# Late odd mamba states worked in the PSUM bank of their decays, half by half, on one Trainium2 core

## The reference, cut to what matters

```
x = x + _L1_attn_ref(_layernorm(x), ...)          # this one
def _mamba(x, ...):                               # once forward, once on the reversed sequence
    dA  = exp(dt[..., None] * A)                  # decays, one plane for each of 16 states
    dBx = (dt * xi)[..., None] * Bm[:, :, None, :]
    def step(h, inp):
        a, bx, c = inp
        h = a * h + bx
        return (h, einsum('bds,bs->bd', h, c))
    y = scan(step, 0, ...) + xi * Dp
    y = y * silu(z)
    return einsum('ble,de->bld', y, out_proj)
```

## Time and profile before

| | us |
|---|---|
| median of 3 runs | 2885.27 (2874.43 to 2886.08) |
| span of the profiled execution | 2872.8 |
| PE busy | 2427.9 (85%) |
| DVE busy | 2361.6 (82%) |
| ACT busy | 1705.4 (59%) |
| POOL busy | 1641.3 (57%) |

### The profile page before, as it was taken

How to read it: one execution, slowest core, us unless ns; L and a number is a source line. 1 busy time by engine, 2 the same in 40 slices (tenths; PEclk the granted TensorE clock), 3 DMA queues, 4 the chain that set the end, 5 groups by cost and what they waited for, 6 DMA issues and landing times.

```text
span 2872.8 us, 30435 instructions
## 1 busy us (share of the span) xinstructions
PE 2427.9 (85%) x8581; PEld 887.3 (31%) x8664; DVE 2361.6 (82%) x3470; ACT 1705.4 (59%) x2859; POOL 1641.3 (57%) x1295
## 2 busy tenths in 40 slices
PE   8777767879789897998889887997879898988888
PEld 3232322323322432233222332232322333333222
DVE  2899899888898999999898989989899987255353
ACT  5666546746749484766658485664638372643444
POOL 2787676756737683867747674776838771121201
PEclk9898967989999898999999898998999899999999
DMA  2333331332313241332323232232413331121111
GB/s 95 107 111 104 104 107 60 100 102 86 100 46 118 86 131 36 110 109 88 117 68 108 96 109 63 96 117 82 135 54 123 93 111 34 56 73 62 32 33 38
DMA packets 159384, 251.29 MB, mean 87 GB/s; under 512 B 20088, under 2 KB 58232, under 8 KB 158960
## 3 DMA queue, kind: packets, MB, share of 16 engines
q1 hardware_dynamic: 159216, 249.34, 27.4%
HBM read 231.71 MB, written 16.50 MB: 86 GB/s over the span
## 4 chain that ended last, share of the span: by engine, by line
DVE 28%; PE 25%; issue 16%; ACT 13%; POOL 12%; SPq 2%; DMA 2%; DVEq 0%; POOLq 0%; ACTq 0%; another core or an unknown queue 0%
PE ps L548 25%; DVE nmx L1336 8%; DVE rh L1416 6%; POOL rb L1838 6%; ACT tN L1722 3%; POOL rh L1828 2%; ACT ps L1777 2%; ACT L1463 2%; DMA cr<-shares 2%; SPq L1939 2%; DVE rh L1422 1%; DVE xib L1402 1%; POOL tF L1859 1%; POOL tF L1852 1%; DVE tF L1253 1%
## 5 line engine op out<-in xcount | busy, mean ns | idle before, releaser
L1416 DVE TENSOR_TENSOR_SCAN rh<-ps,rb 128x512 f32<-128x512 f32 x512 | 619.7, 1215 | 91.0 <-ACT ps L1777 82.4
L1336 DVE TENSOR_REDUCE nmx<-ps 128x1 f32<-128x512 f32 (+3 forms) x864 | 530.5, 661 | 55.1 <-PE ps L548 52.6
L1722 ACT ACTIVATE tN<-ps 128x512 f32<-128x512 f32 (+1 forms) x896 | 463.0, 572 | 136.6 <-PE ps L548 119.5
L548 PE MATMUL ps<-tN,strip 128*64 128x512 f32 (+3 forms) x2048 | 469.9, 549 | 2.5 <-DVE hN L1359 1.8
L1838 POOL TENSOR_TENSOR rb<-duf,bs 128x512 f32<-128x512 f32 x256 | 396.6, 1569 | 131.7 <-DVE rh L1416 129.1
L1828 POOL TENSOR_TENSOR rh<-rh,cs 128x512 f32<-128x512 f32 x208 | 315.3, 1519 | 268.7 <-DVE rh L1416 267.1
L1838 POOL TENSOR_TENSOR rb<-dub,bs 128x512 f32<-128x512 f32 x256 | 388.0, 1534 | 63.0 <-DVE rh L1416 43.5
L548 PE MATMUL ps<-hF,W 128*128 128x512 f32 x592 | 341.9, 661 | 57.0 <-DVE tF L1253 29.7
L548 PE MATMUL ps<-Ks,Qs 128*128 128x512 bf16 (+3 forms) x979 | 291.9, 362 | 74.9 <-DVE nmx L1336 66.7
L1852 POOL TENSOR_TENSOR tF<-tF,cr 128x512 f32<-128x512 f32 x128 | 180.8, 1414 | 275.4 <-DVE tF L1257 154.1
L548 PE MATMUL ps<-tF,W 128*128 128x512 f32 x528 | 283.3, 627 | 21.8 <-POOL tF L1859 11.5
(11 more groups left out here) (259 smaller groups left out, 3672.5 us busy)
## 6 DMA issues: line engine op xcount, KB each, us to landing
cr<-shares SPq DMA_DIRECT2D x248, 256.0 KB, 3.3
bs<-rowsf SPq DMA_DIRECT2D x128, 256.0 KB, 3.6
cs<-rowsf SPq DMA_DIRECT2D x128, 256.0 KB, 3.3
bs<-rowsb SPq DMA_DIRECT2D x128, 256.0 KB, 3.6
cs<-rowsb SPq DMA_DIRECT2D x128, 256.0 KB, 3.3
parts<-spl SPq DMA_DIRECT2D x32, 384.0 KB, 2.8
Qs<-parts SPq DMA_DIRECT2D x384, 32.0 KB
Ks<-parts SPq DMA_DIRECT2D x384, 32.0 KB
```

The costliest lines, as they stand in the source:

```text
L548: return eng.matmul(o, l, r, start=start, stop=stop, skip_group_check=skip_group_check)
L1336: red(nmx[:, 4 * qt + 2 * (i // 4) + a, i % 4:i % 4 + k], o[:, 0:k * nk].rearrange("p (k c) -> p k c", k=k), AX.X, ALU.max, negate=True).t ...
L1416: eng.tensor_tensor_scan(rh[n % NH][:, g, :], decays(n, g), rb[n % NBB][:, g, :], 0.0, ALU.mult, ALU.add).then_inc(s_h, 1)
L1722: act(tN[m % NP][:, a, 0:nq], PA[a][:, 0:nq], ACT.Exp).then_inc(s_ex, 1)
```

## The change

Late states are now handled in pairs of an even state n and the odd one behind it, and the other strands do the same work as before.

- The even state is scanned as before into rh, now rh[n // 2 % 3] (`tile_of`), and its product with C is still POOL's, in a strand C of its own, placed by its own letter in the order.
- The odd state is scanned in place: the scan writes PS, over the decays that it reads. Then, in PS and for the same half, DVE multiplies by C (512 columns), adds the even state's rh (join, 512 columns, counted by the new semaphore s_j) and adds the joined half to xi (512 columns). After that comes the next half.
- ACT's exponential into PS waits, behind an odd half, for this last add and no longer for the scan (`bank_free`).
- rh of a pair is free after the join; the waits of the DMAs and of the block's end follow the new counts.
- l1's product is written to the PSUM tile A instead of y, and the add to X reads it there. In fin the steps go through the PSUM tile PM instead of rM.
- The orders of all engines are new texts. On DVE the S steps grow from 875 to 1187; all other strands have as many steps as before, on every engine.

```diff
+        def pair(n, g):
+            return (n - EARLY) // 2 * 2 + g + 1
+        def in_bank(n):
+            return n >= EARLY and n % 2 == 1
+        def tile_of(n):
+            return n % NH if n < EARLY else n // 2 % NH
+        def times_c_done(n, g=1):
+            if n < EARLY:
+                return s_cv, n + 1
+            return (s_cv, EARLY + pair(n, g)) if in_bank(n) else (s_cp, pair(n, g))
+        def joined(n, g=1):
+            return s_j, pair(n, g)
+        def added(n, g=1):
+            return s_y, n // NS + 1 if n < EARLY else EARLY // NS + pair(n, g)
         def state_free(n):
-            return (s_yp, n + 1) if n < EARLY else added(n)
+            return (s_yp, n + 1) if n < EARLY else joined(n)
+        def bank_free(n, g):
+            m, h = (n, 0) if g else (n - 1, 1)
+            return added(m, h) if in_bank(m) else (s_h, 2 * m + h + 1)
 ...
# DVE, block l1 and fin
-                tt(y, y, A, ALU.mult).then_inc(*k.by_dve(j, "yg"))
+                tt(A, A, y, ALU.mult).then_inc(*k.by_dve(j, "yg"))
-                tt(X[j.b], X[j.b], y, ALU.add).then_inc(*k.by_dve(j, "x"))
+                tt(X[j.b], X[j.b], A, ALU.add).then_inc(*k.by_dve(j, "x"))
-                tt(rM[:, :], y1["f"], PM, ALU.mult).then_inc(*M.by_dve(j, "r1"))
+                tt(PM, PM, y1["f"], ALU.mult).then_inc(*M.by_dve(j, "r1"))
 ...
# DVE, states
+                def scan(n, g, to):
+                    eng.wait_ge(s_a, 2 * n + g + 1)
+                    eng.wait_ge(*times_b_done(n, g))
+                    if not in_bank(n) and n >= NH:
+                        eng.wait_ge(*state_free(n - NH if n < EARLY + 2 * NH else n - 2 * NH))
+                    eng.tensor_tensor_scan(to, decays(n, g), rb[n % NBB][:, g, :], 0.0, ALU.mult, ALU.add).then_inc(s_h, 1)
+                def late_pair(n):
+                    k, p, s = SEQ[n]
+                    for g in range(2):
+                        scan(n, g, rh[tile_of(n)][:, g, :])
+                        yield
+                    for g in range(2):
+                        x = xi[p][:, g, :]
+                        scan(n + 1, g, PS)
+                        yield
+                        eng.wait_ge(s_h, 2 * n + g + 3)
+                        eng.wait_ge(s_cs[(n + 1) % NB], 16 * ((n + 1) // NB + 1))
+                        tt(PS, PS, cs[(n + 1) % NB][:, :], ALU.mult).then_inc(s_cv, 1)
+                        yield
+                        eng.wait_ge(*times_c_done(n, g))
+                        eng.wait_ge(*times_c_done(n + 1, g))
+                        tt(PS, PS, rh[tile_of(n)][:, g, :], ALU.add).then_inc(s_j, 1)
+                        yield
+                        eng.wait_ge(*joined(n, g))
+                        if s == 0:
+                            eng.wait_ge(*jm[k, "m" + p].act("yi1"))
+                        else:
+                            eng.wait_ge(*added(n - 1, g))
+                        tt(x, x, PS, ALU.add).then_inc(s_y, 1)
+                        yield
 ...
# ACT, states
-                        if n:
-                            eng.wait_ge(s_h, 2 * n + g - (n < EARLY))
+                        if n >= EARLY:
+                            eng.wait_ge(*bank_free(n, g))
+                        elif n:
+                            eng.wait_ge(s_h, 2 * n + g - 1)
 ...
# POOL: the products with C of even states
+            def strand_c():
+                for n in range(EARLY, len(SEQ), 2):
+                    for g in range(2):
+                        eng.wait_ge(s_h, 2 * n + g + 1)
+                        eng.wait_ge(s_cs[n % NB], 16 * (n // NB + 1))
+                        h = rh[tile_of(n)][:, g, :]
+                        tt(h, h, cs[n % NB][:, :], ALU.mult).then_inc(s_cp, 1)
+                        yield
```

More of the change, by code:

```diff
@@ L63 @@
+        "P1F8X1F14P1F2P2F2P4F1P3F12X1F6P10X1F10X1F1"
     ),
     "pe": (
[L65 to L68, removed]
@@ L97 @@
+        "X1A2X1A42F16"
     ),
     "dve": (
[L99 to L102 removed]
@@ L173 @@
+        "F18A9F6A1F2A4"
     ),
@@ L1394, in strand_s @@
             def strand_s():
-                def add_state(n):
-                    k, p, s = SEQ[n]
-                    eng.wait_ge(*times_c_done(n))
-                    if s:
-                        eng.wait_ge(*added(n - 1))
-                    else:
-                        eng.wait_ge(*jm[k, "m" + p].act("yi1"))
-                    tt(xi[p][:, :, :], xi[p][:, :, :], rh[n % NH][:, :, :], ALU.add).then_inc(s_y, 1)
                 def add_sum(n):
@@ new lines, in scan, with early @@
+                def scan(n, g, to):
[4 more added lines that the diff above has]
+                    eng.tensor_tensor_scan(to, decays(n, g), rb[n % NBB][:, g, :], 0.0, ALU.mult, ALU.add).then_inc(s_h, 1)
+                def early(n):
+                    for g in range(2):
+                        scan(n, g, rh[n % NH][:, g, :])
+                        yield
+                    eng.wait_ge(s_h, 2 * n + 2)
+                    eng.wait_ge(s_cs[n % NB], 16 * (n // NB + 1))
+                    tt(rh[n % NH][:, :, :], rh[n % NH][:, :, :],
+                       cs[n % NB][:, :].unsqueeze(1).broadcast_to([128, 2, T]), ALU.mult).then_inc(s_cv, 1)
+                    yield
+                    if n % NS == NS - 1:
+                        add_sum(n)
+                        yield
@@ L1437, in strand_f @@
+                for n in range(EARLY):
+                    yield from early(n)
+                for n in range(EARLY, len(SEQ), 2):
+                    yield from late_pair(n)
             def strand_f():
@@ L1822, in strand_s @@
             def strand_s():
-                def times_c(n):
-                    for g in range(2):
-                        eng.wait_ge(s_h, 2 * n + g + 1)
-                        eng.wait_ge(s_cs[n % NB], 16 * (n // NB + 1))
-                        h = rh[n % NH][:, g, :]
-                        tt(h, h, cs[n % NB][:, :], ALU.mult).then_inc(s_cp, 1)
-                        yield
                 for n, (k, p, s) in enumerate(SEQ):
@@ L1839, in strand_s @@
                         yield
-                    if s and not c_dve(n - 1):
-                        yield from times_c(n - 1)
-                    if s == NS - 1 and not c_dve(n):
-                        yield from times_c(n)
+            def strand_c():
+                for n in range(EARLY, len(SEQ), 2):
+                    for g in range(2):
+                        eng.wait_ge(s_h, 2 * n + g + 1)
+                        eng.wait_ge(s_cs[n % NB], 16 * (n // NB + 1))
+                        h = rh[tile_of(n)][:, g, :]
+                        tt(h, h, cs[n % NB][:, :], ALU.mult).then_inc(s_cp, 1)
+                        yield
             def strand_f():
```

254 lines of the change are left out of this document (117 added, 137 removed).

## The result

| | before | after |
|---|---|---|
| median of the runs, us | 2885.68 | 2970.06 (2969.02 to 2979.92) |
| span of the profiled execution, us | 2872.8 | 2967.2 |
| PE busy | 2427.9 (85%) | 2476.5 (83%) |
| DVE busy | 2361.6 (82%) | 2361.6 (80%) |
| ACT busy | 1705.4 (59%) | 1725.7 (58%) |

The changed kernel is slower: the ratio is 1.0315 (95% interval 1.0289 to 1.0340), 85 us or so. The forecast was 2866, its range 2825 to 2925. Several later batches of runs have their own median of the kernel before (2877 to 2881 us); ratios are to that one.

What follows compares the result with a forecast made beforehand. DVE, fullest in the middle stretch (91%), was taken to count nearly in full. DVE -31, bank trips +40, POOL -26 and small steps -2 made -19 us: span 2872.8 to 2854, plus 12.5 gives 2866 us, range 2825 to 2925.

Steps and rivals of the forecast that it cites:

- POOL's relief: POOL's late-state products, free of DVE collisions, run 16% shorter; two thirds of 39 us on the chain, -26 us.
- the new orders: All engines' order texts: said to move the chain, counted only through DVE steps between bank release and next scan.
- DVE time counts nearly in full: Middle stretch: DVE is the fullest engine (91%), so its time counts nearly in full, POOL's in part, ACT's hardly.
- the sum's DVE terms (-31 and +40): DVE's own net time in the late states, -31 us, and its added idle time waiting for the bank, +40 us.
- DVE's durations: Late states on DVE: 479.0 us removed, 624 steps at 679 ns (423.7 us) added, difference -55.3 us.
- rival 4: In-place PSUM steps on DVE take 748 ns instead of 679, +43 us, 2909 us; chance 0.05.
- The gaps: Between DVE steps: free-standing ones overlap by 0.08 us (-25 us), dependent ones start 0.04 us late (+49 us).
- The bank's trips: DVE's idle time before scans while ACT rewrites PS: 82.0 us becomes 114 to 133, taken as +40 us.
- Rival 2: The longer-held bank PS decides: bare trips make 179 us, 97 more than now, 2923 us; chance 0.21.
- rival 1: POOL's gain ends in its own waits for scans, trips cost as taken: +7, 2892 us; chance 0.28 with neighbourhood.
- SP: SP's loads: odd products end later; three buffers cover it, else queued cr loads hold POOL's tF; no term.
- l1 and fin: l1's product and fin's three steps through PSUM: eight batches of four steps, at most 0.15 us each, -2 us.

Runs made afterwards that it cites:

- those two pairs: DVE's 272 expert gate products cut from 512 to 128 columns, in the kernel before (2847.40 us) and in the changed kernel (2933.36 us).
- The faster kernel: The changed kernel with only its five order texts searched anew, for longer: 2893.23 us, ratio 1.0041.
- the first kernel with searched orders for the new work: The changed kernel with only its five order texts searched anew, the shorter search: 2896.04 us, ratio 1.0071.
- run 16: This name does not occur in the text given, which numbers no runs; no change or time can be assigned to it.

## Why the prediction was wrong

Three steps failed: how much DVE time counts, POOL's relief, and above all the new orders, whose own cost the sum put at nothing.

**The bound.** "DVE time counts nearly in full" rested on DVE being the fullest engine. Where DVE work was cut it counted 0.36, before and after. At that rate, an estimate from those two pairs, the sum's DVE terms (-31 and +40) would have come to +3. This changes little of the sum and is not where the 85 us come from. The waits and the zigzag of the chain showed a kernel tied on all sides; I read them, and still took the fullest engine as the path.

**DVE's durations: right where looked for, undone elsewhere.** The late steps were forecast at 679 ns and took 685 to 698: 145.0 + 145.2 + 76.7 + 65.7 = 432.6 us over 104 pairs instead of 423.7, which is -46 against 479.0 where -55 stood. No step passed 700 ns, so rival 4 is out, and the 120 against 58 fixed cycles of the page on VectorE (the Trainium skill, VectorE: DVE Perf Modes, section on the TRN2 errata) don't appear: an add with the other input in PSUM takes 685 ns, the one of two SBUF inputs 688. But DVE's busy time as a whole didn't fall at all. Some 31 us of collision with POOL (34 to 65 us) came on steps that were never mentioned: the small ones of the routers (the tiles whose names begin with sm) took 208.7 us in sum instead of 185.8, the rest is spread. A term for "what POOL now meets instead" was missing.

**The gaps: near.** Scan to product and join to add leave 0.03 to 0.04 us as taken. Product to join leaves 0.10, which is some 11 us more over the stretch. The 0.08 us by which a free-standing step overlaps its predecessor was read wrongly: the two times named for it, 1200.60 + 1.25 and 1201.84, give 0.01. The size is right elsewhere (1230.72 + 0.69 against 1231.33 above), so the term stands.

**The bank's trips: right.** Forecast 114 to 133 us of DVE's idle time before scans, measured 127.1, at 0.84 us a wait where 0.75 was taken, in 152 waits where 179 were counted. The hold alone, measured by itself under SBUF operands, is worth 37 us, near the +40 of the sum. Rival 2 needed 179 us of such waits; its place was right and its price was not reached. Nor does the bank hold the 77 us that new orders gave back: with them DVE still waits 122.4 us for the exponential. What the hold is worth in the changed kernel itself no run shows.

**POOL's relief: right in cause, no effect seen.** Its products fell to 1277 to 1295 ns, as forecast. Of the 26 us nothing is to be seen: POOL's waits for scans before rb rose from 116 to 344 us, while those before rh fell from 267 only to 184. No run gives POOL's relief alone. That was rival 1's mechanism, and I had priced it at nothing coming through (2892), not at a loss.

**The new orders: the term that was left out, and the largest.** The prediction says "a new order moves the chain" and then counts the orders only by the steps between release and scan on DVE. The runs put most of the loss there: same work, other orders, 2970 becomes 2893, and under orders searched alike the two works are equal, as finely as that comparison goes. How the orders do it is shown in part. The faster kernel has 68 us less DVE busy time and the same idle time, and 42 of the 68 us are the excess beside POOL (65 to 23). But DVE's order alone took 53 us off its busy time and brought 9 us at most: idle time came in its place. So fewer collisions go with the gain and are not enough for it. In the middle stretch of after DVE's waits for PE and ACT other than the bank's are each under 17 us, so no single one stands out. Which placements cost what is left open.

**SP.** POOL's waits for the cr loads, named as a danger, rose from 190 to 251 us in the whole run. They are 343 in the first kernel with searched orders for the new work, which is 74 us faster, and 420 in the one with new orders of SP, ACT and POOL, which is as fast as the changed kernel, so they don't explain the loss.

**l1 and fin.** -2 forecast, nothing measured; 2 us is within the noise.

## What to carry over

A busy share of 91% doesn't make an engine the path: before summing its microseconds, look for how much of one counts. Where several engines hold each other by fixed orders it can be far less than all, here 0.36 for two cuts of the same work, and it depends on which work it is. A change that comes with newly written orders has them as its largest unknown; here they moved the same work by 77 us, more than all terms that could be read off the trace. Taking an operand pair out of SBUF does end the collision of these steps with POOL (none of 624 takes over 700 ns), but part of it moves to whatever DVE step stands beside POOL next.

## What the runs showed of the hardware

- A DVE chain in one PSUM bank, read and written in place, costs nearly what the same step costs elsewhere: 697 ns for the product and 698 for the join (in SBUF, undisturbed, 672 to 693), 1227 ns for the scan against 1219 into SBUF.
- A DVE step that depends on the one just before it started 0.03 to 0.04 us after that one's end in scan to product and join to add, and 0.10 us in product to join, with the operands in PSUM as in SBUF; a step that depended on nothing just before it started some 0.08 us before the end.
- Where one DVE instruction lets go both POOL and the next DVE step, two dependent DVE steps with SBUF inputs collide in a fixed pattern: a median of 693 ns (mean 934) for the first and of 1567 (mean 1317) for the second, 672 undisturbed.
- Cutting 151 us of matmul time lowered PE's mean granted clock from 0.924 to 0.894, took 67 us off its busy time and brought no time.
